# x enters the y product in fp32 as it was loaded, and conditioning matrices are fetched by index in every block

## The chip, the cores and the metric

The kernel runs on one core of a Trainium2 chip. The metric is the device time of one execution in microseconds, the median over several runs. The engines of the core are named as in the profile: PE is the matrix engine (TensorE; "PEld" is its weight load), DVE is VectorE, ACT is ScalarE, POOL is GpSimd, SP is the sync engine, which here only issues DMAs.

## The reference

Everything is fp32. B = 64 batches, C = D = 64, T = 1024, 4 experts of rank 8.

```python
y    = einsum('bct,bcd->bdt', x, W[condition])        # W is [16, 64, 64], one matrix for each batch
base = y @ W_up.T                                     # W_up is [1024, 1024]
top1 = argmax(y @ gate_w.T + expert_bias)             # 4 experts
z    = einsum('nh,erh->ner', y, lora_A)               # rank 8
out  = x + base + (z[top1] @ lora_B[top1].T) * 1.0
```

## The kernel before, in words

**Blocks.** The 64 batches are worked on in 16 blocks of four. A block is two row groups t = 0 and 1 of two batches each; a row group of x is 128 partitions (two batches of 64 channels) by 1024 columns. Block 0 is written out by hand in the start-up, together with the preparation of the weights. Blocks 1 to 14 are a loop of seven rounds with two blocks each (`in_blocks`), and block 15, the closing one, follows it. `q` is the number of a block, `par` its parity, and `x_sb` holds x for two blocks.

**The big product.** y @ W_up.T is done in 2x2 form with seven products in place of eight (a11, a12, a22, s1, s2, s3, s4). An operand is split into a high part, rounded to fp32r by ACT (`round_...`, L446), and a low part, the difference, made by DVE (`low_operand`, L873); a product (`multiply`, L680) is three fp32r matmuls for each of four slices. The operands a11, a12, a21, a22 are quarters of y, and s1 to s4 are sums and differences of them, which POOL makes (L286 to L299). DVE adds each product to x in `x_sb` (L960, L964), and SP stores the result. `route` (DVE, small instructions) picks the expert, `turn_z` (L695) transposes the picked z on PE, ACT copies it, and `add_delta` (L686) adds the low-rank term.

**y of the next block.** During block q, PE makes y of block q + 1 in four pieces, `make_y(q + 1, t, h)`, L613 to L622: piece (0,0) after product s2, (0,1) after s1, (1,0) after s3, (1,1) after s4. Their order among the products is written out by hand in the PE's `period`. In the kernel before they go like this:

- x is split into `x_hl`. ACT rounds it to fp32r (`split_x`, L432, one instruction of 64x1024 for each batch), and DVE makes the low part (L863), which lands on the other 64 partitions. So for each batch the 128 partitions of `x_hl` are high and low part of the same 64 channels.
- All 16 conditioning matrices lie in SBUF as `cond_hl`, high and low part side by side, made once in the start-up (L511, L1020).
- PE reads the condition of the batch into a register (`load_index`, L610), and this register picks the matrix in `cond_hl`. A piece is eight fp32r matmuls of 128 columns, `x_hl` as the stationary operand.
- Each batch leaves its result in two column halves that have to be added: ACT copies one to `y_small` (L436), and DVE adds the other (`sum_y`, L868) and so writes a11, a12, a21 or a22.

PE waits before piece (t,0) for `x_low` (DVE's split), and before every piece until the piece before it has been summed out of `y_ps`.

**Block 0 and block 1** get their y in another way (`make_first_y`, L624 to L631): SP fetches the conditioning matrices of two batches by index into a block-diagonal 128x128 tile (`load_first_cond`, L303 to L311), and PE multiplies `x_sb` as loaded, in fp32, by that tile: four matmuls of 128 columns, and ACT copies the bank out (L441).

**Queues.** SP issues the stores of a block in the order c11, c12, c21, c22, each behind a wait for DVE. ACT issues the loads of x for block q + 1 (`load_x`) at the start of block q, each behind a wait for the stores of block q - 1.

Of the kernel before, what the change touches and what calls it, by code (L numbers as in the profile page):

```python
# [5 lines left out]
def adaln_ffn_kernel(  # L6
# [55 lines left out]
    cond_rows = cond_weights.rearrange("s c d -> c s d")  # L62
# [7 lines left out]
    with ctx:  # L70
# [12 lines left out]
        cond_hl = sb("cond_hl", [P, S, 2, D], fp32r)  # L83
# [6 lines left out]
        x_hl = sb("x_hl", [P, 2, 2, T], fp32r)  # L90
        y_small = sb("y_small", [P, BANK], fp32)
# [25 lines left out]
        cond_sb = raw.enter_context(nc.sbuf_tensor("cond_sb", [P, S, D], fp32))  # L117
# [17 lines left out]
        cond_loaded = [sem(f"cond_loaded{h}") for h in range(2)]  # L135
        first_zero = sem("first_zero")
        first_loaded = [sem(f"first_loaded{t}") for t in range(4)]
# [8 lines left out]
        cond_high = sem("cond_high")  # L146
        cond_low = sem("cond_low")
# [7 lines left out]
        x_high = sem("x_high")  # L155
        x_low = sem("x_low")
        y_done = sem("y_done")
        y_small_out = sem("y_small_out")
# [33 lines left out]

        def is_last(q):
            return isinstance(q, int) and q == BLOCKS - 1
# [7 lines left out]
        def halves_of(bank):  # L202
            return bank[:, :, :].rearrange("q n (g a d) -> q (n g) a d", a=2, d=D)
# [5 lines left out]

        def first_cond(t):  # L210
            return y_small[:, t * P:(t + 1) * P]
# [90 lines left out]
        def _(sp):  # L302
            def load_first_cond(t):  # L303
                sp.wait_ge(index_loaded, 16)
                sp.wait_ge(first_zero, 1)
# [15 lines left out]
            load_first_cond(0)  # L321
# [5 lines left out]
            load_first_cond(1)  # L327
# [5 lines left out]
            load_first_cond(2)  # L333
            load_first_cond(3)
# [9 lines left out]
            def period(q, par, closing):  # L344
                sp.wait_ge(c11_out, q + 1)
# [22 lines left out]
        def _(pool):  # L368
# [5 lines left out]
            pool.memset(y_small[:, :], 0.0).then_inc(first_zero, 1)  # L374
# [38 lines left out]
        def _(act):  # L413
# [12 lines left out]
            def split_x(q, par, t, used, halves=(0, 1)):  # L426
                act.wait_ge(x_loaded[2 * par + t], 8 * (q - par) + 16)
                if used:
                    act.wait_ge(y_done, 4 * q - 2 + 2 * t)
                for b in halves:  # L430
                    rows = slice(b * C, (b + 1) * C)
                    act.activation(x_hl[rows, t, b, :], x_sb[rows, 2 * par + t, :], ACT.Copy).then_inc(x_high, 1)  # L432
# [75 lines left out]
            def round_cond():  # L508
                for h in range(2):
                    act.wait_ge(cond_loaded[h], 16)  # L510
                act.activation(cond_hl[:, :, 0, :], cond_sb[:, :, :], ACT.Copy).then_inc(cond_high, 1)  # L511

# [35 lines left out]
            round_cond()  # L548
# [9 lines left out]
            act.wait_ge(cond_low, 1)  # L558
# [19 lines left out]
            def period(q, par, closing):  # L578
# [5 lines left out]
                else:  # L584
# [23 lines left out]
        def _(pe):  # L608
            def load_index(q, t):
                return [pe.value_load(index_sb[0:1, bass.ds(4 * q + 2 * t + b, 1)], min_val=0, max_val=S - 1)  # L610
                        for b in range(2)]
# [557 lines left out]
```

## Time and profile before

| | |
|---|---|
| median of three runs | 432.45 us (432.19 to 432.79) |
| span of the profiled execution, first to last instruction | 430.5 us (430.454) |
| median less span | 2.0 us |
| busy share: PE, DVE, ACT, POOL | 99%, 83%, 44%, 27% |
| chain that ended last | PE 93% of it, `y_ps` L620 11% |
| one block of the loop | 25.2 us |
| granted TensorE clock | 1.00, full speed (2.4 GHz), in all blocks |

No time of its own is given for the profiled execution, only its span; the 2.0 us between it and the median lie around the span. A row of a timeline gives the start and the duration of merged instructions in us. Matmuls overlap in the pipeline, so the time that a group of them takes on PE is read from its start to the start of the next group, and is shorter than the printed duration.

### The profile page before, as it was taken

Reading aid. Unit: us, or ns where it says so; the run is one execution under the profiler, and the core shown is the slowest. Engines: PE = TensorE matmul, PEld = TensorE weight load, DVE = VectorE, ACT = ScalarE, POOL = GpSimd, SP = SyncE. Lnnn points to the kernel's source line nnn. Section 1 sums busy time; section 2 is a strip of 40 time slices with the busy share of each in tenths; the row PEclk is TensorE's granted clock in tenths of the full one; section 3 lists DMA queues with packets and bytes.
Section 4 is the critical chain, followed back from the end, with each engine's and each line's share of the span. In section 5 each row is a group of like instructions: output and inputs, shape, how many; then the busy total and the mean of one; then the engine's idle time right before and its main releaser. Section 6 shows DMA issues by size and latency. Waiting matters only on the chain.

```text
span 430.5 us, 8609 instructions
## 1 busy us (share of the span) xinstructions
PE 424.8 (99%) x2937; PEld 396.7 (92%) x2938; DVE 358.1 (83%) x648; ACT 191.5 (44%) x302; POOL 117.5 (27%) x92
## 2 busy tenths in 40 slices
PE   8999999999999999999999999999999999999997
PEld 7989999999999999999999999999999999999996
DVE  3998489697979979797997979799797989979773
ACT  4873463362625336262543636254263625426220
POOL 4971040503205050220505023050502305050230
DMA  7930140402214041230503123050312305031202
GB/s 266 350 57 3 48 151 24 151 33 90 96 41 154 24 129 41 90 105 32 163 24 124 46 78 117 24 171 24 122 49 72 123 24 171 24 122 49 80 19 97
DMA packets 18583, 38.85 MB, mean 90 GB/s; under 512 B 5095, under 2 KB 5351, under 8 KB 18571
## 3 DMA queue, kind: packets, MB, share of 16 engines
q1 hardware_dynamic: 14336, 23.86, 15.8%
q10 hardware_dynamic: 4234, 14.83, 11.4%
q8 instruction: 7, 0.11, 0.1%
q14 instruction: 6, 0.04, 0.0%
HBM read 21.91 MB, written 16.78 MB: 90 GB/s over the span
## 4 chain that ended last, share of the span: by engine, by line
PE 93%; ACT 3%; DMA 2%; DVE 1%; SPq 0%; issue 0%; DVEq 0%
PE bank_x L680 23%; PE bank_y L680 23%; PE bank_c L680 20%; PE y_ps L620 11%; PE bank_b L680 10%; DMA w_raw<-in_L_ffn_W_up_dram 2%; PE bank_x L686 1%; PE bank_y L686 1%; PE bank_b L686 1%; PE bank_c L686 1%; PE y_ps L628 1%; ACT w_s L493 1%; ACT w_a L493 1%; PE bank_y L717 1%; PE bank_y L663 1%; PE bank_c L695 1%
## 5 line engine op out<-in xcount | busy, mean ns | idle before, releaser
L286 POOL TENSOR_TENSOR s_sum<-a 128x512 f32<-128x512 f32 x15 | 19.5, 1301 | 283.3 <-DVE a L868 264.8
L432 ACT ACTIVATE x_hl<-x_sb 64x1024 fp32r<-64x1024 f32 x56 | 59.1, 1055 | 34.0 <-DMA out_dram<-x_sb 29.4
L863 DVE TENSOR_TENSOR x_hl<-x_sb,x_hl 64x1024 fp32r<-64x1024 f32 x56 | 68.4, 1221 | 1.7
L436 ACT ACTIVATE y_small<-y_ps 128x512 f32<-128x512 f32 x56 | 33.5, 598 | 57.7 <-PE y_ps L620 57.7
L620 PE MATMUL y_ps<-cond_hl,x_hl 128*128 x448 | 58.1, 273 | 0.0
L620 PEld LDWEIGHTS y_ps<-cond_hl,x_hl 128*128 128x128 f32 x448 | 54.7, 191 | 1.5
L680 PE MATMUL bank_x<-w_a,hl_a 128*128 128x256 f32 (+1 forms) x408 | 54.2, 288 | 0.0
L680 PEld LDWEIGHTS bank_x<-w_a,hl_a 128*128 128x128 f32 x408 | 52.9, 188 | 0.4
L868 DVE TENSOR_TENSOR a<-y_ps,y_small 128x512 f32<-128x512 f32 x56 | 38.5, 687 | 16.7 <-ACT y_small L436 16.7
L680 PE MATMUL bank_y<-w_s,hl_s 128*128 128x292 f32 (+1 forms) x384 | 51.6, 290 | 0.0
L680 PE MATMUL bank_x<-w_s,hl_s 128*128 128x292 f32 (+1 forms) x384 | 51.5, 290 | 0.0
L680 PE MATMUL bank_y<-w_a,hl_a 128*128 128x292 f32 (+1 forms) x384 | 51.0, 288 | 0.0
L680 PEld LDWEIGHTS bank_y<-w_s,hl_s 128*128 128x128 f32 x384 | 49.9, 188 | 0.8 <-issue 0.2
L680 PEld LDWEIGHTS bank_x<-w_s,hl_s 128*128 128x128 f32 x384 | 49.8, 188 | 0.6
L680 PEld LDWEIGHTS bank_y<-w_a,hl_a 128*128 128x128 f32 x384 | 49.6, 188 | 0.1
L680 PE MATMUL bank_c<-w_s,hl_s 128*128 128x512 f32 x192 | 48.2, 399 | 0.0
L680 PE MATMUL bank_b<-w_s,hl_s 128*128 128x512 f32 x192 | 48.2, 400 | 0.0
L446 ACT ACTIVATE hl_a<-a 128x512 fp32r<-128x512 f32 x48 | 30.5, 636 | 36.1 <-DVE a L868 33.6
L680 PEld LDWEIGHTS bank_c<-w_s,hl_s 128*128 128x128 f32 x192 | 34.9, 188 | 7.3
L680 PEld LDWEIGHTS bank_b<-w_s,hl_s 128*128 128x128 f32 x192 | 35.2, 190 | 6.8
L680 PE MATMUL bank_c<-w_a,hl_a 128*128 128x512 f32 x168 | 41.2, 394 | 0.0
L873 DVE TENSOR_TENSOR hl_s<-s_sum,hl_s 128x512 fp32r<-128x512 f32 x32 | 37.8, 1188 | 4.0 <-ACT hl_s L446 3.1
(120 smaller groups left out, 566.0 us busy)
## 6 DMA issues: line engine op xcount, KB each, us to landing
out_dram<-x_sb SPq DMA_DIRECT2D x63, 256.0 KB, 2.0
x_sb<-in_x_dram ACTq DMA_DIRECT2D x28, 512.0 KB, 3.7
w_raw<-in_L_ffn_W_up_dram SPq DMA_DIRECT2D x8, 512.0 KB, 7.5
x_sb<-in_x_dram SPq DMA_DIRECT2D x4, 512.0 KB, 8.8
cond_sb<-in_L_cond_weights_dram SPq DMA_DIRECT2D x2, 256.0 KB, 10.1
out_dram<-x_sb SPq DMA_DIRECT2D x2, 128.0 KB, 1.9
router_sb<-in_L_ffn_lora_A_dram ACTq DMA_DIRECT2D x1, 128.0 KB
lora_b_sb<-in_L_ffn_lora_B_dram SPq DMA_DIRECT2D x1, 128.0 KB, 7.8
```

Of the source, the lines that this page charges most:

```text
L286: eng.tensor_tensor(s1_sum[:, :], a21[:, :], a22[:, :], ALU.add).then_inc(s1_added, 1)
L432: act.activation(x_hl[rows, t, b, :], x_sb[rows, 2 * par + t, :], ACT.Copy).then_inc(x_high, 1)
L436: act.activation(y_small[:, :].rearrange("q (g d) -> q g d", d=D), halves_of(y_ps)[:, :, 1, :], ACT.Copy).then_inc(y_small_out, 1)
L446: act.activation(hl[op][:, 0, :, :], src[:, :].rearrange("q (k n) -> q k n", n=P), ACT.Copy)\
L493: act.activation(turn_target(op, c, 0), bank.rearrange("q (k n) -> q k n", n=P), ACT.Copy)\
L620: mm = pe.matmul(y_ps[:, k % KH // 2, at:at + P], x_hl[:, t, b, k * P:(k + 1) * P], cond_hl[:, index[b], :, :], start=True, stop=True)
L628: mm = pe.matmul(FIRST_Y[2 * t + h][:, k * P:(k + 1) * P], x_sb[:, t, (h * KH + k) * P:(h * KH + k + 1) * P], first_cond(t), start=True, s ...
L680: mm = pe.matmul(dst, hl[op][:, a, k, :], w[:, b, k, cols], start=(fresh and k == 0 and a + b == 0), stop=(k == KH - 1 and a == 1), skip_g ...
L686: return pe.matmul(dst, z_t[t][:, :], src, start=False, stop=True, skip_group_check=True)
L863: dve.tensor_tensor(x_hl[other, t, b, :], x_sb[rows, 2 * par + t, :], x_hl[rows, t, b, :].bitcast(fp32), ALU.subtract).then_inc(x_low, 1)
L868: dve.tensor_tensor(dst[:, :].rearrange("q (g d) -> q g d", d=D), halves_of(y_ps)[:, :, 0, :], y_small[:, :].rearrange("q (g d) -> q g d", ...
L873: dve.tensor_tensor(hl[op][:, 1, :, :], src[:, :].rearrange("q (k n) -> q k n", n=P), hl[op][:, 0, :, :].bitcast(fp32), ALU.subtract).then ...
```

## The change

The y of every block is made as that of the first two: x as loaded, in fp32, times a block-diagonal pair of conditioning matrices. The split of x (ACT and DVE), the register loads on PE, the resident `cond_hl` with its loads and splits, and the sum over halves on DVE are gone. The 128x128 tiles now lie in `cond_pair`, four of them (two blocks, two row groups), cleared once by POOL. SP fetches the four matrices of block q + 1 at the start of its `period` for block q, so behind the stores of block q - 1 and ahead of those of block q. A piece of y is four fp32 matmuls; PE waits before piece (t,0) for x and for the pair, and before every piece until all pieces but the last one have been moved. ACT moves a piece out of `y_ps` directly (`move_y`).

```diff
-        x_hl = sb("x_hl", [P, 2, 2, T], fp32r)
-        y_small = sb("y_small", [P, BANK], fp32)
+        cond_pair = sb("cond_pair", [P, 4, P], fp32)
...
 # SyncE
+            def load_pair(q, par, t):
                 for b in range(2):
                     rows = slice(b * C, (b + 1) * C)
-                    index = sp.value_load(index_sb[0:1, 2 * t + b:2 * t + b + 1], min_val=0, max_val=S - 1)
-                    sp.dma_start(first_cond(t)[rows, b * D:(b + 1) * D],
+                    index = sp.value_load(index_sb[0:1, bass.ds(4 * q + 2 * t + b, 1)], min_val=0, max_val=S - 1)
+                    sp.dma_start(cond_pair[rows, 2 * par + t, b * D:(b + 1) * D],
                                  cond_weights[bass.ds(index, 1), :, :].rearrange("s c d -> (s c) d"))\
-                       .then_inc(first_loaded[t], 16)
+                       .then_inc(pair_loaded[2 * par + t], 16)
+            def load_next_pair(q, par, t):
+                sp.wait_ge(y_done, 4 * q + 2 * t - 6)
+                load_pair(q, par, t)
...
             sp.dma_start(x_sb[:, 2, :], x_pairs[2]).then_inc(x_loaded[2], 16)
-            sp.dma_start(cond_sb[0:C, :, :], cond_rows).then_inc(cond_loaded[0], 16)
             sp.dma_start(x_sb[:, 3, :], x_pairs[3]).then_inc(x_loaded[3], 16)
-            sp.dma_start(cond_sb[C:2 * C, :, :], cond_rows).then_inc(cond_loaded[1], 16)
...
             def period(q, par, closing):
+                if q_next(q):
+                    load_next_pair(q + 1, 1 - par, 0)
+                    load_next_pair(q + 1, 1 - par, 1)
                 sp.wait_ge(c11_out, q + 1)
                 store(q, par, 0, 0)
 # ScalarE
-            def split_x(q, par, t, used, halves=(0, 1)):
...
-            def move_small_y(q, t, h):
+            def move_y(q, t, h, to):
                 act.wait_ge(y_done, 4 * q + 2 * t + h + 1)
-                act.activation(y_small[:, :].rearrange("q (g d) -> q g d", d=D), halves_of(y_ps)[:, :, 1, :],
-                               ACT.Copy).then_inc(y_small_out, 1)
+                act.activation(to[:, :], y_ps[:, h, :], ACT.Copy).then_inc(y_summed, 1)
...
-            round_cond()
-            act.wait_ge(cond_low, 1)
...
-                    split_x(q + 1, 1 - par, 0, True)
                 round_s4(q, True)
                 round_s3(q, True)
-                if not closing:
-                    split_x(q + 1, 1 - par, 1, True)
                 move_z(q, par, 0, True)
                 if not closing:
-                    move_small_y(q + 1, 0, 0)
+                    move_y(q + 1, 0, 0, a11)
                     round_a11(q + 1, True)
-                    move_small_y(q + 1, 0, 1)
+                    act.wait_ge(low["s4"], q + 1)
+                    move_y(q + 1, 0, 1, a12)
                     round_a12(q + 1, True)
-                    move_small_y(q + 1, 1, 0)
+                    move_y(q + 1, 1, 0, a21)
                 move_z(q, par, 1, True)
                 if not closing:
-                    move_small_y(q + 1, 1, 1)
+                    move_y(q + 1, 1, 1, a22)
                     round_a22(q + 1, True)
 # TensorE
-            def load_index(q, t):
...
-            def make_y(q, t, h, index):
+            def make_y(q, par, t, h):
                 if h == 0:
-                    pe.wait_ge(x_low, 4 * q + 2 * t - 6)
-                pe.wait_ge(y_summed, 4 * q + 2 * t + h)
-                for k in range(h * KH, (h + 1) * KH):
-                    for b in range(2):
-                        at = (k % 2) * 2 * P + b * P
-                        mm = pe.matmul(y_ps[:, k % KH // 2, at:at + P], x_hl[:, t, b, k * P:(k + 1) * P],
-                                       cond_hl[:, index[b], :, :], start=True, stop=True)
+                    pe.wait_ge(x_loaded[2 * par + t], 8 * (q - par) + 16)
+                    pe.wait_ge(pair_loaded[2 * par + t], 16 * (q - par) + 32)
+                pe.wait_ge(y_summed, 4 * q + 2 * t + h - 1)
+                for k in range(KH):
+                    mm = pe.matmul(y_ps[:, h, k * P:(k + 1) * P],
+                                   x_sb[:, 2 * par + t, (h * KH + k) * P:(h * KH + k + 1) * P],
+                                   cond_pair[:, 2 * par + t, :], start=True, stop=True)
                 mm.then_inc(y_done, 1)
 # VectorE
-            def split_x(q, par, t, b):
-            def sum_y(dst, q, t, h):
-            def split_cond():
...
```

## Rows read from the trace of the kernel before

**Rows 1.** The page, busy time, share and instructions of each engine.
```profile
PE 424.8 (99%) x2937; PEld 396.7 (92%) x2938; DVE 358.1 (83%) x648; ACT 191.5 (44%) x302; POOL 117.5 (27%) x92
```

**Rows 2.** Windows of blocks 2, 8 and 15: length, busy by engine, clock, DMA.
```profile
77.52:103.05 25.52, 25.52 (x173) 23.61 (x172) 21.48 (x39) 11.18 (x18) 5.91 (x4) 1.00 0.25 84
...
229.04:254.25 25.20, 25.20 (x173) 23.54 (x172) 21.87 (x39) 11.30 (x18) 6.25 (x4) 1.00 0.25 83
...
405.45:430.45 25.00, 22.17 (x153) 20.51 (x151) 15.46 (x33) 3.88 (x8) 5.85 (x4) 1.00 0.20 74
```

**Rows 3.** Timeline of PE in block 8, the four pieces (L620) and what follows.
```profile
240.91 1.00 PE L620 MATMUL y_ps<-cond_hl,x_hl 128*128 x8
...
241.80 3.00 PE L680 MATMUL bank_b<-w_s,hl_s 128*128 128x512 f32 x12
...
244.88 1.00 PE L620 MATMUL y_ps<-cond_hl,x_hl 128*128 x8
245.72 3.24 PE L680 MATMUL bank_x<-w_s,hl_s 128*128 128x292 f32 x24
248.80 1.06 PE L620 MATMUL y_ps<-cond_hl,x_hl 128*128 x8
249.69 3.01 PE L680 MATMUL bank_c<-w_s,hl_s 128*128 128x512 f32 x12
...
252.77 0.27 PE L695 MATMUL bank_y<-ident,z_parts 128*128 128x128 f32 x1
...
254.02 0.39 PE L686 MATMUL bank_b<-lora_b_hl,z_t 128*128 128x512 f32 x1
```

**Rows 4.** Timeline of PE in the start-up, pieces of y in fp32 (L628).
```profile
12.94 1.06 PE L628 MATMUL y_ps<-y_small,x_sb 128*128 128x128 f32 x8
13.83 0.60 PE L663 MATMUL bank_b<-ident,w_raw 128*128 128x128 f32 x4
...
27.37 0.60 PE L663 MATMUL y_ps<-ident,w_raw 128*128 128x128 f32 x4
27.72 3.01 PE L680 MATMUL bank_b<-w_s,hl_s 128*128 128x512 f32 x12
...
42.04 1.06 PE L628 MATMUL y_ps<-y_small,x_sb 128*128 128x128 f32 x8
42.85 3.04 PE L680 MATMUL bank_c<-w_s,hl_s 128*128 128x512 f32 x12
...
50.83 0.27 PE L695 MATMUL bank_y<-ident,z_parts 128*128 128x128 f32 x1
...
52.07 0.39 PE L686 MATMUL bank_b<-lora_b_hl,z_t 128*128 128x512 f32 x1
```

**Rows 5.** Timelines of DVE and PE in block 2, around piece (1,0).
```profile
96.17 1.22 DVE L863 TENSOR_TENSOR x_hl<-x_sb,x_hl 64x1024 fp32r<-64x1024 f32 x1
...
97.53 1.12 PE L620 MATMUL y_ps<-cond_hl,x_hl 128*128 x8
```

**Rows 6.** Timelines of PE and DVE in block 15, around product s2.
```profile
408.46 3.20 PE L680 MATMUL bank_x<-w_a,hl_a 128*128 128x292 f32 x24
411.67 3.27 PE L680 MATMUL bank_y<-w_s,hl_s 128*128 128x292 f32 x24
414.79 0.33 PE L695 MATMUL bank_c<-ident,z_parts 128*128 128x128 f32 x1
...
410.29 2.92 DVE L873 TENSOR_TENSOR hl_s<-s_sum,hl_s 128x512 fp32r<-128x512 f32 x2 [0.83 <-ACT hl_s L446]
```

**Rows 7.** The page, DVE's sum of y: count, busy us, mean ns, idle before.
```profile
L868 DVE TENSOR_TENSOR a<-y_ps,y_small 128x512 f32<-128x512 f32 x56 | 38.5, 687 | 16.7 <-ACT y_small L436 16.7
```

**Rows 8.** Timeline of SP: a pair fetched, stores in block 8; landing of pairs.
```profile
10.04 1.72 SPq L309 DMA_DIRECT2D y_small<-in_L_cond_weights_dram  x2
...
230.83 0.91 SPq L337 DMA_DIRECT2D out_dram<-x_sb  x2
...
DMA to landing us min/median/max: 2.4/5.9/7.0
```

More of the change, by code:

```diff
@@ L116, in adaln_ffn_kernel @@
         raw.enter_context(nc.sbuf_tensor("raw_rest", [P, KH * 2 * GC - OC * ER], fp32))
-        cond_sb = raw.enter_context(nc.sbuf_tensor("cond_sb", [P, S, D], fp32))
         raw.close()
@@ L134, in adaln_ffn_kernel @@
         bias_zero = sem("bias_zero")
-        cond_loaded = [sem(f"cond_loaded{h}") for h in range(2)]
-        first_zero = sem("first_zero")
-        first_loaded = [sem(f"first_loaded{t}") for t in range(4)]
+        pair_zero = sem("pair_zero")
+        pair_loaded = [sem(f"pair_loaded{s}") for s in range(4)]
         index_loaded = sem("index_loaded")
@@ L191, in in_blocks, with q_next @@
             period(BLOCKS - 1, (BLOCKS - 1) % 2, True)
+        def q_next(q):
+            return not isinstance(q, int) or 0 < q < BLOCKS - 1
         def is_last(q):
@@ L320, in _ @@
             load_w_up(4)
-            load_first_cond(0)
+            load_first_pair(0, 0)
             sp.dma_start(x_sb[:, 0, :], x_pairs[0]).then_inc(x_loaded[0], 16)
@@ L326, in _ @@
             load_w_up(1)
-            load_first_cond(1)
+            load_first_pair(0, 1)
             sp.dma_start(x_sb[:, 1, :], x_pairs[1]).then_inc(x_loaded[1], 16)
             sp.dma_start(x_sb[:, 2, :], x_pairs[2]).then_inc(x_loaded[2], 16)
-            sp.dma_start(cond_sb[0:C, :, :], cond_rows).then_inc(cond_loaded[0], 16)
             sp.dma_start(x_sb[:, 3, :], x_pairs[3]).then_inc(x_loaded[3], 16)
-            sp.dma_start(cond_sb[C:2 * C, :, :], cond_rows).then_inc(cond_loaded[1], 16)
-            load_first_cond(2)
-            load_first_cond(3)
+            load_first_pair(1, 0)
+            load_first_pair(1, 1)
             def store(q, par, t, half):
@@ L373, in _ @@
             pool.memset(bias_sb[:, :], 0.0).then_inc(bias_zero, 1)
-            pool.memset(y_small[:, :], 0.0).then_inc(first_zero, 1)
+            pool.memset(cond_pair[:, :, :], 0.0).then_inc(pair_zero, 1)
             for e in range(E):
@@ L424, in load_x @@
                 act.dma_start(x_sb[:, 2 * par + t, :], x_pairs[2 * q + t]).then_inc(x_loaded[2 * par + t], 16)
-            def split_x(q, par, t, used, halves=(0, 1)):
[L427 to L432, printed above, removed]
-            def move_small_y(q, t, h):
+            def move_y(q, t, h, to):
                 act.wait_ge(y_done, 4 * q + 2 * t + h + 1)
-                act.activation(y_small[:, :].rearrange("q (g d) -> q g d", d=D), halves_of(y_ps)[:, :, 1, :],
-                               ACT.Copy).then_inc(y_small_out, 1)
+                act.activation(to[:, :], y_ps[:, h, :], ACT.Copy).then_inc(y_summed, 1)
             def move_first_y(n, to):
@@ L506, in move_z @@
                 act.activation(z_t[t][:, :], src, ACT.Copy).then_inc(z_ready, 1)
[L508 to L511, printed above, removed]
             act.wait_ge(ident_done, 1)
@@ L625, in make_first_y @@
                 pe.wait_ge(x_loaded[t], 16)
-                pe.wait_ge(first_loaded[t], 32)
+                pe.wait_ge(pair_loaded[t], 32)
                 for k in range(KH):
                     mm = pe.matmul(FIRST_Y[2 * t + h][:, k * P:(k + 1) * P],
-                                   x_sb[:, t, (h * KH + k) * P:(h * KH + k + 1) * P], first_cond(t),
+                                   x_sb[:, t, (h * KH + k) * P:(h * KH + k + 1) * P], cond_pair[:, t, :],
                                    start=True, stop=True)
@@ L821, in period @@
                 multiply("a11", q, chain, True)
-                index = [None, None]
-                if not closing:
-                    index[0] = load_index(q + 1, 0)
                 pe.wait_ge(c21_out, q)
@@ L832, in period @@
                 if not closing:
-                    make_y(q + 1, 0, 0, index[0])
+                    make_y(q + 1, 1 - par, 0, 0)
                     pe.wait_ge(p4_out, q)
@@ L839, in period @@
                 if not closing:
-                    make_y(q + 1, 0, 1, index[0])
+                    make_y(q + 1, 1 - par, 0, 1)
                 pe.wait_ge(u2_out, q + 1)
@@ L843, in period @@
                 if not closing:
-                    index[1] = load_index(q + 1, 1)
-                    make_y(q + 1, 1, 0, index[1])
+                    make_y(q + 1, 1 - par, 1, 0)
                 multiply("s4", q, bank_c, True)
@@ L851, in period @@
                 else:
-                    make_y(q + 1, 1, 1, index[1])
+                    make_y(q + 1, 1 - par, 1, 1)
                     pe.wait_ge(u3_out, q + 1)
@@ L859, in _ @@
         def _(dve):
-            def split_x(q, par, t, b):
-                rows, other = slice(b * C, (b + 1) * C), slice((1 - b) * C, (2 - b) * C)
-                dve.wait_ge(x_high, 4 * q + 2 * t + b - 7)
-                dve.tensor_tensor(x_hl[other, t, b, :], x_sb[rows, 2 * par + t, :],
-                                  x_hl[rows, t, b, :].bitcast(fp32), ALU.subtract).then_inc(x_low, 1)
-            def sum_y(dst, q, t, h):
-                dve.wait_ge(y_small_out, 4 * q + 2 * t + h - 7)
-                dve.tensor_tensor(dst[:, :].rearrange("q (g d) -> q g d", d=D), halves_of(y_ps)[:, :, 0, :],
-                                  y_small[:, :].rearrange("q (g d) -> q g d", d=D), ALU.add).then_inc(y_summed, 1)
             def low_operand(op, src, q):
@@ L1016, in after_delta22 @@
                 add_bank(bank_b, par, 1, 1).then_inc(c22_out, 1)
-            def split_cond():
-                dve.wait_ge(cond_high, 1)
-                dve.tensor_tensor(cond_hl[:, :, 1, :], cond_sb[:, :, :], cond_hl[:, :, 0, :].bitcast(fp32),
-                                  ALU.subtract).then_inc(cond_low, 1)
             split_turned("s4", 2)
@@ L1067, in _ @@
             low_operand("s4", a12, 0)
-            split_cond()
             after_p6(0, 0)
@@ L1104, in period @@
                 if not closing:
-                    for b in range(2):
-                        split_x(q + 1, 1 - par, 0, b)
                     after_p4(q, par)
@@ L1113, in period @@
                 else:
-                    sum_y(a11, q + 1, 0, 0)
-                    split_x(q + 1, 1 - par, 1, 0)
                     low_operand("a11", a11, q + 1)
@@ L1119, in period @@
                 if not closing:
-                    sum_y(a12, q + 1, 0, 1)
-                    split_x(q + 1, 1 - par, 1, 1)
                     low_operand("a12", a12, q + 1)
@@ L1124, in period @@
                 route(q, 1)
-                if not closing:
-                    sum_y(a21, q + 1, 1, 0)
                 after_delta12(q, par)
                 if not closing:
-                    sum_y(a22, q + 1, 1, 1)
                     after_delta21(q, par)
```

21 lines of the change are left out of this document (4 added, 17 removed).

## The prediction

> **What bounds the kernel now.** I read the page's engine line first: PE is busy 424.8 of 430.5 us, DVE 83%, ACT 44% [rows 1]. Then the windows, block by block: in a block of the loop PE is busy for its whole length, 25.20 of 25.20 us, at a granted clock of 1.00, which is the upper level, 2.4 GHz [rows 2]. So what counts is what PE does in its own stream, and the few places where it waits. Busy time hides such waits here, because a matmul's printed duration covers its neighbour's start. I therefore take the time of a piece of y from its start to the start of the next group, in the timeline [rows 3]. Two places stand out in the windows: block 2 takes 25.52 us where block 8 takes 25.20, and in the closing block PE is busy only 22.17 of 25.00 us [rows 2].
>
> The change takes four instructions for each row group from DVE and two from ACT. None of that shortens the kernel by itself: DVE and ACT are not the bound. It counts only where PE waits for them.
>
> **The change, part by part.**
>
> *The pieces of y on PE.* Before, a piece is eight matmul records. The four pieces of block 8 take: (0,0) with the transpose of z behind it, 241.80 - 240.91 = 0.89 us; (0,1) 245.72 - 244.88 = 0.84; (1,0) 249.69 - 248.80 = 0.89; and (1,1) with the transpose ahead of it and a pair of delta matmuls behind it, 254.02 - 252.77 = 1.25 [rows 3]. That is 3.87 us for each block.
>
> The new piece has the same form as the pieces of the start-up, which are in the trace: four fp32 matmuls of 128 columns, that show as eight records, x_sb the stationary operand [rows 4]. So halving the number of matmuls in the code does not halve the work. With a product behind, such a piece takes 42.85 - 42.04 = 0.81 us; with a fp32 transpose behind, 13.83 - 12.94 = 0.89; and from the transpose of z over piece and delta pair it is 52.07 - 50.83 = 1.24 [rows 4]. A transpose ahead of a product costs little of its own: four take 27.72 - 27.37 = 0.35, so three at 0.11 and the last 0.03 [rows 4]. The product behind a fp32 piece starts up some 0.03 us slower (s4's duration is 3.04 us behind a fp32 piece, 3.01 behind the other form [rows 3, 4]). The four places after the change:
> - (0,0): 0.89 + 0.03 = 0.92, against 0.89: +0.03
> - (0,1): 0.81 + 0.03 = 0.84, against 0.84: 0
> - (1,0): 0.81 + 0.03 = 0.84, against 0.89: -0.05
> - (1,1): 1.24 against 1.25: -0.01
>
> The sum is -0.03 us for a block, and 14 blocks (1 to 14) make such pieces: 14 x 0.03 = -0.4 us. These are differences of hundredths, so I bound the term by 0 and by twice its size, -0.8.
>
> The precision page of the Trainium skill (FP8 and Floating Point Precision, TensorE Precision Notes) says that true fp32 takes four passes through the array, where reduced fp32 takes one, which speaks against this change. The trace does not show it as time for this shape: the fp32 piece takes 0.81 us, the one before 0.84. By the pass count alone, half the matmuls with four passes each would double the array's work in the pieces.
>
> *Block 2.* It is 25.52 - 25.20 = 0.32 us longer than block 8 [rows 2]. At piece (1,0) DVE's last half of the split of x ends at 96.17 + 1.22 = 97.39 and PE starts the piece at 97.53 [rows 5]; in the code the piece waits for that split (`x_low`). With the split gone PE waits for the loaded x only, which is what the split itself had to have before it. I take the full -0.3 us; the other bound is 0.
>
> *The closing block.* Product a12 there takes 411.67 - 408.46 = 3.21 us, and a11 ahead of it, the same 24 matmuls, 408.46 - 405.45 = 3.01 [rows 2, 6]. Behind a12 comes s2 with no a22 between, and its low part is made by DVE only from 410.29 on, after 0.83 us of waiting for ACT's rounding, which waits for POOL's s1 and s2, and these for the last piece of y [rows 6]. s2 then takes 414.79 - 411.67 = 3.12, another 0.11 too much. Now ACT's copy is the last step of y and DVE's addition, 0.69 us [rows 7], falls out of this chain, so the low part comes about 0.7 us earlier, more than the 0.3 us that PE loses. What is late next is the transpose of z, which needs DVE's routing behind the low parts; it moves forward with them. I take -0.3 us, bounds 0 and -0.4.
>
> *The start-up.* Two 256 KB loads and a rounding and a split of 128x1024 go. In the code they are issued behind all of W_up and behind x of row groups 0 to 2, so nothing that PE needs early is queued behind them; I count 0, and as bounds one stall of the size of block 2's, -0.3, and +0.1.
>
> *SP.* Four fetches for each block. SP has nothing to do between the last store of block 7, issued by 230.83 + 0.91 = 231.74 [rows 8], and the first of block 8, which comes only behind s1 and the first delta pair, so close to 244.88, where the piece behind them starts [rows 3]. Two fetches take 1.72 us from issue to issue's end, and with the register load ahead of the first some 2.5 [rows 8]: 5 us for the four, all in that gap. Queued behind them is only that store. The pair for (0,*) is issued by 234.3; in the start-up such a fetch landed 2.4 to 7.0 us after issue, median 5.9, behind the loads of W_up [rows 8]. So it lands between 236.7 and 241.3, most likely near the lower end since only two stores are ahead of it; PE wants it at 240.91 [rows 3]. The second pair is issued by 236.8 and wanted at 248.80. Cost 0; at the upper bound of 7.0 it would be 0.4 us in each block.
>
> The DMA page of the Trainium skill (DMA: Bandwidth & Descriptors, Anatomy of one DMA) gives about 2.0 us as the fixed cost of one DMA on another path than this; 2.4 us, the fastest here, is near it, and by that figure no pair would be late.
>
> *ACT's copy, PE's waits, register loads.* The copy is as long as that to `y_small`, and hidden. PE has one more semaphore wait for each row group and two register loads fewer; its sequencer runs ahead of the array, 0.
>
> **Sum.** -0.4 - 0.3 - 0.3 = -1.0 us: a span of 430.5 - 1.0 = 429.5, and with the 2.0 us around it, against the median of 432.45, 431.4 us. As a ratio it is -0.23%. The measurement tells about 0.2% (0.9 us) from no change, so the forecast lies just past that bound. The case's own range comes from the term bounds, not all at an end together: 430.9 to 432.1.
>
> **The rivals.**
> - *Nothing that can be told.* The pieces come out equal in the blocks, and only one of the two stalls goes; 0 to -0.5 us, 432.2. For it: the piece term is a sum of hundredths and one of its four parts is positive. Against it: both stalls have their cause in the removed work. Chance 0.24.
> - *The pairs come late.* The mechanism is the landing on SP's queue, behind two stores. It decides from a landing of 6.6 us on (234.3 + 6.6 = 240.9); at 7.0 it is 0.4 us in each of 14 blocks: +5.6 - 1.0, so 437. Against it is the missing W_up traffic. Chance 0.05.
> - *fp32 costs its passes.* A one-pass matmul of the piece takes 0.84 / 8 = 0.105 us; four times that for four matmuls is 1.68, +0.84 for each of 56 pieces: +47 us, 479. The rows of the start-up exclude it nearly: 0.01. (By the rule of the precision page.)
> - *PE's sequencer loses its lead* at three waits in a row ahead of (t,0), where two stood: if each shows as some 0.1 us, a record's pace, it costs 28 x 0.1 = +2.8 against -1.0, 434.3. Against it: with two waits the pieces show nothing of that size. Chance 0.06.
> - *A larger gain.* Every term comes at its lower bound: -0.8 in the pieces, -0.3 in block 2, -0.4 in the closing block, -0.3 in the start-up, together -1.8 us, 430.6. For it: DVE, with 56 x 1.22 = 68 us [rows 5] and 38.5 us [rows 7] less to do, is in time everywhere. Chance 0.09.
>
> That leaves 0.55 for the forecast.
>
> **Chances and range.** The forecast's case falls past -0.9 us in about three of five: 0.34; with the larger gain 0.43, and some of the no-change case's spread makes it 0.46. Slower: 0.05 + 0.01 + 0.06 and 0.01 of spread, 0.13. Same: 0.41. The range for 8 in 10: down past the larger gain, 430.3, up past no change, 432.9; what it leaves out is the three slower rivals and a little of the spread at both ends, under 0.2.
>
> **What would show it.** PE in a middle block: 25.17 us for 25.20; piece (0,1) to its product 0.81; (0,0) with the transpose 0.92. Block 2 as long as the others. In block 15, a12 3.0 us. `cond_pair` landings of 2 to 4 us, and no wait of PE for them. DVE's busy share near 58% ((358.1 - 68 - 38.5) / 430). The prediction is wrong if the eight records of a fp32 piece pace at another step than 0.11 us in the loop, if the 0.3 us of block 2 stay (then it is not the split), or if blocks carry a new wait for `cond_pair` or x.

## The result: 431.08 us, 1.2 us less than before

The changed kernel takes 431.08 us (median of 16 runs, 430.94 to 432.29), the kernel before 432.26 (16 runs). The ratio is 0.9971, 95% interval 0.9961 to 0.998. The profiled execution has a span of 429.3 us against 430.5, at a granted clock of 1.00.

The page of the changed kernel, busy time and share by engine, then the times from issue to landing of SP's fetches:

```profile
PE 423.2 (99%) x2937; PEld 395.8 (92%) x2937; DVE 264.4 (62%) x535; ACT 134.3 (31%) x245; POOL 113.4 (26%) x92
...
cond_pair<-in_L_cond_weights_dram SPq DMA_DIRECT2D x64, 16.0 KB, 2.6
```

DVE has 94 us less to do than in [rows 1] and ACT 57, and the kernel is 1.2 us shorter; PE has as many instructions as before. The windows of blocks 2, 8 and 15 of the changed kernel, with the columns of [rows 2]:

```profile
77.41:102.58 25.17, 25.17 (x173) 23.48 (x172) 15.25 (x32) 7.21 (x14) 5.92 (x4) 1.00 0.26 88
228.43:253.60 25.17, 25.17 (x173) 23.51 (x172) 15.24 (x32) 7.28 (x14) 5.92 (x4) 1.00 0.26 86
404.63:429.28 24.65, 21.85 (x153) 20.45 (x151) 15.08 (x32) 3.94 (x8) 5.84 (x4) 1.00 0.20 75
```

So block 2 is 0.35 us shorter, block 8 0.03, and the closing block 0.35. Read from the first product of a block to that of the next, all 14 blocks of the loop now take 25.16 to 25.18 us, where before 13 of them took 25.19 to 25.22 and block 2 25.52. The difference of the spans, 1.17 us, is made up as: start-up up to block 1, 52.30 to 52.25, -0.05; block 2 -0.355; the other 13 blocks together -0.41; closing block -0.35.

The timeline of PE in block 8 of the changed kernel answers to [rows 3]:

```profile
240.29 1.05 PE L593 MATMUL y_ps<-cond_pair,x_sb 128*128 128x128 f32 x8
241.18 0.27 PE L669 MATMUL bank_c<-ident,z_parts 128*128 128x128 f32 x1
241.21 2.99 PE L654 MATMUL bank_b<-w_s,hl_s 128*128 128x512 f32 x12
...
244.28 1.05 PE L593 MATMUL y_ps<-cond_pair,x_sb 128*128 128x128 f32 x8
245.08 3.28 PE L654 MATMUL bank_x<-w_s,hl_s 128*128 128x292 f32 x24
248.20 1.05 PE L593 MATMUL y_ps<-cond_pair,x_sb 128*128 128x128 f32 x8
249.01 3.04 PE L654 MATMUL bank_c<-w_s,hl_s 128*128 128x512 f32 x12
...
252.12 0.27 PE L669 MATMUL bank_y<-ident,z_parts 128*128 128x128 f32 x1
...
253.37 0.40 PE L660 MATMUL bank_b<-lora_b_hl,z_t 128*128 128x512 f32 x1
```

From starts: piece (0,0) with the transpose 0.92 us, (0,1) 0.80, (1,0) 0.81, and the group around (1,1) 1.25. Before they were 0.89, 0.84, 0.89 and 1.25 [rows 3]. Only (1,0) keeps a gain: the product behind (0,1) takes 248.20 - 245.08 = 3.12 where it took 248.80 - 245.72 = 3.08, which gives the gain of (0,1) back. Of (1,0)'s own 0.08 us the product s4 behind it gives back 0.03: both together take 252.12 - 248.20 - 0.23 = 3.69 us, where they took 252.77 - 248.80 - 0.23 = 3.74 (0.23 is the delta matmul between s4 and the transpose). The closing block, PE's timeline, answers to [rows 6]:

```profile
404.63 3.19 PE L654 MATMUL bank_y<-w_a,hl_a 128*128 128x292 f32 x24
407.66 3.19 PE L654 MATMUL bank_x<-w_a,hl_a 128*128 128x292 f32 x24
410.68 3.19 PE L654 MATMUL bank_y<-w_s,hl_s 128*128 128x292 f32 x24
413.71 0.27 PE L669 MATMUL bank_c<-ident,z_parts 128*128 128x128 f32 x1
413.74 3.00 PE L654 MATMUL bank_b<-w_s,hl_s 128*128 128x512 f32 x12
```

a12 takes 3.02 us in place of 3.21, s2 3.03 in place of 3.12, and the transpose of z, up to the product behind it, 0.03 in place of 0.10. These three make up the 0.35 us.

### The profile page after: what moved, and what is told of

It is laid out like the page before. It is cut to its first block, busy times and chain, and to the rows that moved or that the text cites. A ratio compares the mean times of both kernels' runs of the same rounds, so it can differ in the third digit from the quotient of the medians.

```text
span 429.3 us, 8491 instructions
## 1 busy us (share of the span) xinstructions
PE 423.2 (99%) x2937; PEld 395.8 (92%) x2937; DVE 264.4 (62%) x535; ACT 134.3 (31%) x245; POOL 113.4 (26%) x92
## 4 chain that ended last, share of the span: by engine, by line
PE 93%; ACT 3%; DMA 2%; DVE 1%; SPq 0%; issue 0%; DVEq 0%
PE bank_x L654 23%; PE bank_y L654 23%; PE bank_c L654 19%; PE y_ps L593 12%; PE bank_b L654 10%; DMA w_raw<-in_L_ffn_W_up_dram 2%; PE bank_y L660 1%; PE bank_x L660 1%; PE bank_b L660 1%; PE bank_c L660 1%; PE y_ps L602 1%; ACT w_s L480 1%; ACT w_a L480 1%; PE bank_y L691 1%; PE bank_y L637 1%; ACT lora_b_hl L478 0%
## 5 line engine op out<-in xcount | busy, mean ns | idle before, releaser
L831 DVE TENSOR_TENSOR hl_a<-a,hl_a 128x512 fp32r<-128x512 f32 x49 | 39.5, 806 | 41.6 <-ACT hl_a L433 41.6
L593 PE MATMUL y_ps<-cond_pair,x_sb 128*128 128x128 f32 x448 | 59.0, 275 | 0.0
L424 ACT ACTIVATE a<-y_ps 128x512 f32<-128x512 f32 x56 | 33.4, 597 | 80.1 <-PE y_ps L593 80.1
L593 PEld LDWEIGHTS y_ps<-cond_pair,x_sb 128*128 128x128 f32 x448 | 54.6, 191 | 1.3
L831 DVE TENSOR_TENSOR hl_s<-s_sum,hl_s 128x512 fp32r<-128x512 f32 x32 | 48.4, 1548 | 0.3 <-ACT hl_s L433 0.2
L922 DVE TENSOR_TENSOR x_sb<-bank_c,x_sb 128x512 f32<-128x512 f32 x30 | 20.7, 691 | 33.2 <-PE bank_c L660 26.3
L918 DVE TENSOR_TENSOR x_sb<-bank_y,x_sb 128x512 f32<-128x512 f32 x39 | 26.7, 684 | 16.4 <-PE bank_y L660 8.5
L654 PEld LDWEIGHTS bank_c<-w_a,hl_a 128*128 128x128 f32 x168 | 30.6, 188 | 6.1
```

What stands on the lines that cost most here:

```text
L424: act.activation(to[:, :], y_ps[:, h, :], ACT.Copy).then_inc(y_summed, 1)
L593: mm = pe.matmul(y_ps[:, h, k * P:(k + 1) * P], x_sb[:, 2 * par + t, (h * KH + k) * P:(h * KH + k + 1) * P], cond_pair[:, 2 * par + t, :], ...
L654: mm = pe.matmul(dst, hl[op][:, a, k, :], w[:, b, k, cols], start=(fresh and k == 0 and a + b == 0), stop=(k == KH - 1 and a == 1), skip_g ...
L831: dve.tensor_tensor(hl[op][:, 1, :, :], src[:, :].rearrange("q (k n) -> q k n", n=P), hl[op][:, 0, :, :].bitcast(fp32), ALU.subtract).then ...
L918: return dve.tensor_tensor(wide(x_part(par, t, half)), bank[:, :, 0:QUARTER], wide(x_part(par, t, half)), ALU.add)
L922: return dve.tensor_tensor(x_part(par, t, half), bank[:, 0, :], x_part(par, t, half), ALU.add)
```

## The experiments

The table gives for each run the length of block 2, of the other 13 blocks of the loop, and of the closing block, from its trace, in us. The start-up is left out of it: in all but one of these traces the first loop block begins between 52.2 and 52.6 us, whatever the edit, so differences of 0.3 us in a span can come from there. The exception is e7. The kernel before was run again beside each set of experiments: 432.28 us beside e1 to e4, 432.35 beside e5 to e8, 432.30 beside e9 to e12. Ratios are to these.

| run | block 2 | other blocks | closing | median (runs) |
|---|---|---|---|---|
| before | 25.52 | 25.19 to 25.22 | 25.00 | 432.26 (16) |
| changed | 25.17 | 25.16 to 25.18 | 24.65 | 431.08 (16) |
| e1 before, no split | 25.17 | 25.14 to 25.20 | 25.01 | 431.91 (10) |
| e2 before, no index | 26.29 | 25.17 to 25.21 | 24.99 | 432.83 (1) |
| e3 changed, split and wait back | 25.17 | 25.16 to 25.18 | 24.65 | 431.25 (10) |
| e4 changed, split back | 25.17 | 25.16 to 25.18 | 24.66 | 431.16 (1) |
| e5 changed, one DVE step in y's chain | 25.17 | 25.16 to 25.18 | 25.02 | 431.59 (10) |
| e6 changed, half the columns | 25.15 | 25.15 to 25.21 | 24.66 | 431.02 (1) |
| e7 changed, double the columns | 28.55 | 28.54 to 28.55 | 24.66 | 482.03 (1) |
| e8 changed, pairs behind a22 | 26.72 | 26.72 to 27.14 | 24.66 | 454.66 (1) |
| e9 before, split ahead of the sums | 26.96 | 26.19 to 26.36 | 25.01 | 446.99 (4) |
| e10 changed, splits and sums back | 26.26 | 25.19 to 25.22 | 25.02 | 432.94 (10) |
| e11 changed, pairs behind a12 | 25.18 | 25.16 to 25.18 | 24.65 | 431.17 (1) |
| e12 changed, other start-up order | 25.17 | 25.16 to 25.17 | 24.66 | 431.39 (11) |

**e1: the kernel before without the split in the loop.**

```diff
-                    split_x(q + 1, 1 - par, 0, True)
...
+                    act.activation(x_hl[:, t, b, :]..., ident..., ACT.Copy)
...
-                    pe.wait_ge(x_low, 4 * q + 2 * t - 6)
+                    pe.wait_ge(x_loaded[2 * par + t], 8 * (q - par) + 16)
```

> The kernel before, with the split of x left out of the loop: x_hl is filled once in the start-up and the pieces of y multiply that, so y is not the reference's; PE waits for the loaded x in place of the split. Theory (PE waits for DVE's split): block 2 falls from 25.52 to 25.20 us or less, piece (1,0) from 0.87-0.90 to about 0.84-0.87, so the other blocks fall by up to 0.03; the closing block stays at 25.00, since the sum on DVE stays. Median about -0.6 us against before. Rival (the register loads on PE or the fp32r form make these times): block 2 stays at 25.5 and (1,0) as it is; no change in the median.

DVE's calls of `split_x` in the loop are gone as well. Ratio 0.9994 (0.9977 to 1.0012). The blocks say more than the median: PE's timeline around piece (1,0) of a middle block, and the window of block 2.

```profile
248.56 1.00 PE L621 MATMUL y_ps<-cond_hl,x_hl 128*128 x8
249.40 1.38 PE L681 MATMUL bank_c<-w_s,hl_s 128*128 128x512 f32 x5
```
```profile
77.75:102.92 25.17, 25.17 (x173) 23.48 (x172) 17.22 (x35) 7.14 (x14) 5.91 (x4) 1.00 0.24 85
```

With fp32r matmuls and resident matrices as before, and register loads too, (1,0) takes 0.84 us, block 2 25.17 and the mean block the same 25.17 as in the changed kernel. So the gain of the loop does not need the fp32 form. The closing block kept its 25.01. The median came 0.37 us lower (431.91 against 432.28) where I had expected 0.6: this profile's start-up was 0.26 us longer than that of before. That most likely comes from the experiment itself: the four added ACT instructions hold ACT for 3.89 us from 34.75 on, and the stretch of PE from 35.8 to 45.9 us, which they run beside, takes 10.16 us, where it takes 9.84 to 9.85 in every other trace.

**e2: the kernel before without register loads.**

```diff
-                                       cond_hl[:, index[b], :, :], start=True, stop=True)
+                                       cond_hl[:, b, :, :], start=True, stop=True)
```

> The kernel before, with the register loads on PE left out: each batch uses matrix 0 or 1 of the resident set, so y is not the reference's. Theory: nothing moves, block 2 stays at 25.52, (1,0) at 0.87-0.90, the block at 25.20, the closing block at 25.00. Rival (register loads cost): (1,0), which follows a load, falls to 0.84, blocks by 0.03 or more.

I had expected no change; outside block 2, piece (1,0) fell to 0.84 to 0.88, and the blocks to a mean of 25.18, half of the way to 25.17. So the registers, the loads or the addressing with them, have a part in the 0.03 us for each block, but only together with the late split: in e1 and in e9 (below) they stand as before, the split is gone or early, and (1,0) takes 0.84 in every block. This is one execution. Block 2 went up to 26.29, which says what sort of stall this is. ACT's timeline there: it waited 4.03 us for a store to land before it could issue the load of x that stands ahead of the split in its queue.

```profile
85.84 0.34 ACTq L424 DMA_DIRECT2D x_sb<-in_x_dram  x1
86.31 2.15 ACT L432 ACTIVATE x_hl<-x_sb 64x1024 fp32r<-64x1024 f32 x2 [4.03 <-DMA out_dram<-x_sb]
```

The stall of block 2 is thus not a fixed 0.3 us. It is how far stores that land late, in one execution, push the splits of x past PE's need. In the kernel before too it stands at both row groups. DVE's timeline, then PE's, at piece (0,0) of block 2:

```profile
86.77 2.47 DVE L863 TENSOR_TENSOR x_hl<-x_sb,x_hl 64x1024 fp32r<-64x1024 f32 x2
```
```profile
89.38 1.11 PE L620 MATMUL y_ps<-cond_hl,x_hl 128*128 x8
```

The split ends at 89.24, 0.14 us ahead of the piece; in the blocks after it, it ends 0.88 ahead. Piece (0,0) and the two groups behind it are 0.15 us longer than in the other blocks, and s3 with (1,0) 0.17 us.

**e3 and e4: the split back in the changed kernel, with and without PE's wait.**

```diff
+                    split_x(q + 1, 1 - par, 0)            # ACT and DVE, at their old places
...
                     pe.wait_ge(pair_loaded[2 * par + t], 16 * (q - par) + 32)
+                    pe.wait_ge(x_low, 4 * q + 2 * t - 6)  # e3 only
```

> The changed kernel with the split of x put back on ACT and DVE, into a tile that no product reads, and with PE waiting for it before pieces (0,0) and (1,0), as before. Theory: block 2 goes from 25.17 back to 25.5, (1,0) longer by some 0.03-0.07 in each block; the closing block stays at 24.65, because no sum on DVE is in its chain. Median +0.6 to +0.9 us against the changed kernel. Rival (the fp32 form made the gain): blocks stay at 25.17.

> The same as the run with the wait, but PE does not wait for the split: only the work is back on ACT and DVE. Theory: the load alone costs nothing, all blocks 25.17, closing 24.65 to 24.7. Rival (it was the load of ACT and DVE, through a shared port or late low parts): blocks longer, up to 25.2, block 2 up to 25.5, closing up to 25.0.

e4 came as expected: no change. e3 did not: ratio 0.9978 (0.9965 to 0.9992), and not one block longer, though PE waits for the split as it did before. My theory up to here, that the wait for the split is what costs, falls in this form. DVE's timeline of e3 with PE's shows why; the last two lines are DVE's and PE's in block 8 of the kernel before:

```profile
191.65 1.22 DVE L846 TENSOR_TENSOR x_hl<-x_sb,x_hl 64x1024 fp32r<-64x1024 f32 x1
...
195.16 1.22 DVE L846 TENSOR_TENSOR x_hl<-x_sb,x_hl 64x1024 fp32r<-64x1024 f32 x1
```
```profile
197.80 1.05 PE L607 MATMUL y_ps<-cond_pair,x_sb 128*128 128x128 f32 x8
```
```profile
247.38 1.22 DVE L863 TENSOR_TENSOR x_hl<-x_sb,x_hl 64x1024 fp32r<-64x1024 f32 x1
```
```profile
248.80 1.06 PE L620 MATMUL y_ps<-cond_hl,x_hl 128*128 x8
```

The last half of the split ends at 196.38, 1.4 us ahead of the piece. In the kernel before it ended at 248.60 for the piece at 248.80, 0.2 us ahead, and in block 2 at 97.39 for a piece at 97.53 [rows 5]. The difference of 1.2 us is what the two sums of y that stood ahead of it in DVE's queue take there, at 0.6 us from start to start. The new theory: splits are late because they are queued behind sums, which wait for PE and ACT. e9 and e10 test it.

**e5: one DVE step put back into the chain of the last piece.**

```diff
-                    move_y(q + 1, 1, 1, a22)
+                    act.activation(y_hop[:, :], y_ps[:, 1, :], ACT.Copy).then_inc(y_hop_out, 1)
...
+                    dve.tensor_tensor(a22[:, :], y_hop[:, :], y_hop[:, :], ALU.max).then_inc(y_summed, 1)
```

> The changed kernel with one DVE instruction of 128x512 put back into the chain of the last piece: ACT copies piece (1,1) into a tile, DVE copies that into a22. Theory (closing term: DVE's addition in the chain y, s1, s2, rounding, low part): the closing block goes from 24.65 back to 24.9-25.0, product a12 there from 3.02 to about 3.2; all other blocks 25.17. Median +0.3 us. Rival (the closing gain came from DVE having less to do overall): closing stays at 24.65.

```profile
407.75 3.18 PE L657 MATMUL bank_x<-w_a,hl_a 128*128 128x292 f32 x24
410.98 3.27 PE L657 MATMUL bank_y<-w_s,hl_s 128*128 128x292 f32 x24
414.10 0.33 PE L672 MATMUL bank_c<-ident,z_parts 128*128 128x128 f32 x1
```

The closing block is 25.02 us again, a12 3.23, s2 3.12, and all other blocks 25.17. The ratio, 0.9986 (0.9957 to 1.0015), is too wide to show it, the trace does: one instruction of 0.69 us in the chain from the last piece over s1 and s2 to the low part costs 0.37 us there, and nothing in the loop, where a22 stands between a12 and s2.

**e6 and e7: half and double the moving columns.**

```diff
-                                   cond_pair[:, 2 * par + t, :], start=True, stop=True)
+                                   cond_pair[:, 2 * par + t, 0:D], start=True, stop=True)                # e6, output slice to match
+                                   cond_pair[:, 2 * par + t, :].unsqueeze(1).to_broadcast([P, 2, P]), ...)  # e7, likewise
```

> The changed kernel with 64 moving columns in place of 128 in each matmul of the loop's pieces (half of y left out, so the output is not the reference's). Theory (the weight load sets the pace of a record): records stay 0.111 us apart, a piece 0.80, blocks within 0.1 us of 25.17. Rival (the passes set it: two of 128 columns for each record are 0.107 us at 2.4 GHz): records 0.055-0.06 apart, a piece about 0.45, block 23.7, median -20 us.

> The changed kernel with 256 moving columns in each matmul of the loop's pieces (the pair's tile twice; the writes overlap in the bank, so y is not the reference's). Theory (weight load of 0.111 us, or the stream where it is longer): a record at 256 columns takes two passes of 256, 0.21 us, so a piece about 1.7 us and a block 25.17 + 4 x 0.9 = 28.8. Rival (a record is one pass): 256 columns are 0.107 us, records stay near 0.12 apart, a block about 25.3.

PE's timeline of e6, piece (1,0), and then of e7, piece (0,0), each with what follows:

```profile
248.21 1.00 PE L593 MATMUL y_ps<-cond_pair,x_sb 128*128 128x64 f32 x8
249.02 3.05 PE L654 MATMUL bank_c<-w_s,hl_s 128*128 128x512 f32 x12
```
```profile
210.47 1.89 PE L594 MATMUL y_ps<-cond_pair,x_sb 128*128 128x256 f32 x8
212.20 0.27 PE L670 MATMUL bank_c<-ident,z_parts 128*128 128x128 f32 x1
```

Half the columns leave the piece at 0.81 us: the stream of columns is not what paces a record of 64 or 128 columns. The weight load, one for each record, is the candidate; it was not varied by itself. Double the columns make the piece ahead of the transpose 1.73 us where it was 0.89, and the pieces with a product or a delta pair behind them 1.54 where they were 0.81. A record then takes 0.216 us, which at 2.4 GHz is the time of about 512 columns, 256 twice. The Trainium skill (FP8 and Floating Point Precision, TensorE Precision Notes) gives four passes for true fp32. The trace agrees: two passes for each of the two records of a matmul. By that count, an estimate, the passes take 0.107 us for a record at 128 columns, and hide within the 0.111 us that a record takes with 64 columns as well. With twice the columns a block is 3.4 us longer: 3.0 in the pieces, the rest in what stands behind them. I had expected 3.6. The 482 us of e7 also hold a start-up 3.6 us longer, ahead of all that the edit touches: PE waits 1.8 us there for a load of W_up, and then the granted clock is 0.50, the level of 1.2 GHz, from 10.5 to 13.0 us, where it is 1.00 throughout in the changed kernel.

**e8 and e11: the pairs fetched later.**

```diff
                 if q_next(q):
+                    sp.wait_ge(product_done["a22"], q + 1)      # e8; "a12" in e11
                     load_next_pair(q + 1, 1 - par, 0)
```

> The changed kernel with SP waiting for product a22 of the block before it fetches the pairs. a22 ends 8.9 us into a block, the first pair is issued 2.5 us later and lands 2.4-2.6 us after that, at 14.0; PE wants it at 12.1. Theory: every block has a wait of some 1.9 us at piece (0,0), block about 27.1, median +26 us. Rival (the pairs are hidden anyway, or land faster): no change.

> The changed kernel with SP waiting for product a12 of the block, 6.1 us into it, before it fetches the pairs. First pair issued by 8.6, landed by 11.2, wanted at 12.1. Theory: no wait, blocks 25.17. With the run behind a22 this brackets the point from which lateness costs. Rival (landing 3.5 us or more): blocks 25.2 to 25.8.

```profile
200.26 1.15 PE L594 MATMUL y_ps<-cond_pair,x_sb 128*128 128x128 f32 x8 [1.28 <-DMA cond_pair<-in_L_cond_weights_dram]
```

Behind a22, which ends 8.8 us into a block, blocks are 1.5 to 2.0 us longer, all of it at piece (0,0); behind a12, which ends at 6.1, nothing is lost. In the changed kernel the first fetch is issued 2.8 us into the block (231.24 - 228.43, SP's timeline):

```profile
231.24 4.52 SPq L295 DMA_DIRECT2D cond_pair<-in_L_cond_weights_dram  x4
```

With the register load ahead of it that is a start at about 1.8. So a delay of some 4.3 us is free, and one of 7.0 costs 1.5 to 2.0: the room is about 5 us.

**e9: the kernel before, split ahead of the sums.**

```diff
-                    sum_y(a11, q + 1, 0, 0)
                     split_x(q + 1, 1 - par, 1, 0)
+                    split_x(q + 1, 1 - par, 1, 1)
+                    sum_y(a11, q + 1, 0, 0)
                     low_operand("a11", a11, q + 1)
...
                     sum_y(a12, q + 1, 0, 1)
-                    split_x(q + 1, 1 - par, 1, 1)
```

> The kernel before with two moves in DVE's order alone: both halves of the split for row group 1 go ahead of the sum for a11 (they stood behind the sums for a11 and a12, which wait for a piece of y and for ACT's copy). New theory (it is not the split's work nor PE's wait for it, but that the split stands in DVE's queue behind the sums): the last half ends some 2 us before piece (1,0), (1,0) takes 0.84 in all blocks, blocks 25.17, block 2 25.17 to 25.2, closing block unchanged at 25.00; median about -0.7 us against before. Rival (the split's own length, or the load of DVE): blocks stay at 25.20 and block 2 at 25.5.

It is slower by 3.4% (1.0319 to 1.0351). DVE's timeline, then PE's:

```profile
223.89 2.47 DVE L863 TENSOR_TENSOR x_hl<-x_sb,x_hl 64x1024 fp32r<-64x1024 f32 x2
226.39 0.69 DVE L868 TENSOR_TENSOR a<-y_ps,y_small 128x512 f32<-128x512 f32 x1
```
```profile
225.95 0.40 PE L686 MATMUL bank_x<-lora_b_hl,z_t 128*128 128x256 f32 x2
227.14 1.11 PE L620 MATMUL y_ps<-cond_hl,x_hl 128*128 x8 [0.79 <-DVE a L868]
228.09 3.12 PE L680 MATMUL bank_y<-w_s,hl_s 128*128 128x292 f32 x23
```

The forecast of -0.7 us was wrong, though one part of it held: (1,0) takes 0.84 us in every block. But the sum for a11 now ends at 227.08, and PE waits for it before piece (0,1), since both banks of `y_ps` are read by one sum: about 1 us in each block. The order of before was pinned from both sides, the sum by piece (0,1) and the split by (1,0), with no room for 2.4 us between.

**e10: splits and sums back, in the fp32 form.**

```diff
-                pe.wait_ge(y_summed, 4 * q + 2 * t + h - 1)
+                pe.wait_ge(y_summed, 4 * q + 2 * t + h)
...
+                    hop_y(a11, q + 1, 0, 0)               # DVE, 128x512, for each piece at the old sum's place
+                    split_x(q + 1, 1 - par, 1, 0)
...
```

> The changed kernel in fp32, with the split back (PE waits for it) and with a DVE instruction of 128x512 for each piece at the place and in the order of the old sums. New theory (sums ahead of splits on DVE make them late; the form of the matmul is neutral): (1,0) longer than 0.81 by 0.02 to 0.06, blocks 25.20, block 2 25.3 to 25.5, closing 25.0: the time of before, median 432.3. Rival (the fp32 form is what made it robust): blocks at 25.17.

Beside what is shown, PE's wait for `x_low` is back as in e3, and ACT's wait for s4's low part ahead of the copy of piece (0,1), which only the changed kernel has, is gone. Ratio 1.0013 (0.9998 to 1.0027). Windows of blocks 2, 8 and 15, then PE's timeline in block 2:

```profile
77.49:103.75 26.26, 25.69 (x173) 23.57 (x172) 21.89 (x39) 11.27 (x18) 6.24 (x4) 1.00 0.26 84
229.75:254.96 25.20, 25.20 (x173) 23.55 (x172) 21.90 (x39) 11.28 (x18) 6.24 (x4) 1.00 0.26 86
406.19:431.21 25.02, 22.17 (x153) 20.50 (x151) 15.45 (x33) 3.93 (x8) 5.85 (x4) 1.00 0.20 74
```
```profile
89.86 1.16 PE L608 MATMUL y_ps<-cond_pair,x_sb 128*128 128x128 f32 x8 [0.35 <-DVE x_hl L847]
```

All three gains are gone: blocks 25.20, (1,0) 0.85, closing 25.02, and a stall in block 2, here 1.1 us, at the splits of both row groups. Two waits of PE are back at (1,0), for the split and for the sum of the piece before. It is the split that ends last: in the middle blocks 0.19 us ahead of the piece, the sum 1.44 us. So with splits and sums the loop takes the time of before in either form of the matmul, and each block is 0.03 us shorter without the split in fp32r (e1), and with the split but without the sums in fp32 (e3). The closing block's part was taken out and put back in the fp32 form only (e5); a fp32r kernel without the sum was not run.

Block 2 is less clear. In e10 DVE stands idle there before the split of the first row group:

```profile
87.33 2.47 DVE L847 TENSOR_TENSOR x_hl<-x_sb,x_hl 64x1024 fp32r<-64x1024 f32 x2 [1.33 <-ACT x_hl L432]
```

So it is not a sum that holds this split up, but ACT, which waited 3.96 us for a store and could issue its load of x only at 85.77; in e3's profile that load went out at 83.50. How e3 would fare with stores as late as these, its trace doesn't show. Its ten executions speak for no stall in most: 8 have a span of 429.2 to 429.4 us. Those of e10 would be near 430.0 without a stall in block 2 (an estimate from the other blocks and the closing one), and 6 of 10 are 430.9 or more.

**e12: an attempt at a faster one.** PE has one stall left in the changed kernel that DVE causes, 0.36 us in the start-up before the last transposes for a22.

```diff
-            split_turned("s2", 1)
-            low_operand("s2", s2_sum, 0)
             subtract(dve, 4, 3)
+            split_turned("s2", 1)
+            low_operand("s2", s2_sum, 0)
```

> The changed kernel with DVE's last subtraction of W_up quarters (for the transpose a22, 3, which PE waits for at 31.9 us in the start-up) ahead of the last split of s2 and the low part of s2. Theory: PE's stall of 0.36 us there goes, and s2's product does not become late: span 428.9 to 429.0, median -0.3 us against the changed kernel. Rival: s2's low part becomes the bound instead, and nothing is won.

```profile
30.55 0.60 PE L637 MATMUL bank_c<-ident,w_raw 128*128 128x128 f32 x4
31.66 0.66 PE L637 MATMUL y_ps<-ident,w_raw 128*128 128x128 f32 x4 [0.51 <-DVE w_s L852]
```

Neither theory had it right. The stall did not go, it moved forward and grew: from the transposes at 30.55 to the next it is 1.11 us, four at a pace of 0.11 would be 0.44, and these next ones need a bank of `y_ps` that the moved split of s2 frees. The ratio to before is 0.998 (0.9971 to 0.9989), no better than the changed kernel, and the start-up is 0.24 us longer than there.

## Why the prediction was right

- *The sum.* Predicted -1.0 us on the span, measured -1.17; predicted 431.4 us, measured 431.08, in the range. As a ratio -0.29% against -0.23%. Two of the three terms, block 2 and the closing block, came from waits that the prediction had named and that the experiments bear out. The third had the right size for another reason.
- *Pieces on PE*, -0.03 us for a block: measured 25.20 to 25.17, -0.41 over 13 blocks. The total is right, its parts are not: all of it is (1,0), and e1 shows that to be the end of a wait and not a cheaper piece. The prediction took the 0.89 us of (1,0) as the price of the form and did not ask why (0,1), the same form, took 0.84. That +0.03, 0, -0.05 and -0.01 added up to the measured sum is in part luck. That eight records cost the same in both forms held: (1,0) and s4 together take 3.69 us in fp32 (changed) and in fp32r (e1).
- *Block 2*, -0.3: measured -0.35. That the split is behind it is right (e1). The reason was incomplete: it named piece (1,0) alone, where only half of the stall stands, the other half being at (0,0). What starts it is a store that lands late and holds up ACT's load and split of x (e2, e10); it was 0.3 us in one execution and 1.1 in two others. With the split back but no sums (e3) there was no stall; how much of that is the shorter queue on DVE and how much a store that landed earlier, the runs don't separate.
- *Closing block*, -0.3: measured -0.35, and e5 brings 0.37 of it back with one instruction. The shift of 0.7 us was more than the loss, as worked out, and the transpose of z moved forward too, 0.10 to 0.03 us, as foreseen.
- *Start-up*, 0: 52.30 to 52.25 us, within the 0.4 us by which start-ups differ here. Not shown to be anything else than 0.
- *SP*, 0: the four fetches are issued by 235.76, 7.3 us into the block, and land in 2.6; no wait of PE for them. The rival of late pairs was real in kind, with its point at some 5 us of delay (e8, e11), not reached.
- *fp32's passes*: the rival was rightly put at 0.01 for 128 columns, but only because a record takes that long with half the columns too; e7 shows the price.
- *DVE's share* was to be near 58%, and is 62%, 13 us more than worked out. The low parts of s1 and s2 take 1.55 us on average in place of 1.19, which is 11 of them; no run tests why. The blocks take their 25.17 us all the same.
- *The sequencer's lead*: one wait more for each row group shows nothing; each of the four pieces has the same length in all 14 blocks, within 0.001 us.

## What to carry to other kernels

Where PE is 99% busy, 94 us less work on DVE is worth only what PE waited for, and such waits do not show as idle time: compare the lengths of equal blocks and of equal groups from start to start, and look at the blocks that stand out. Then ask not only what the late instruction costs but what stands ahead of it in its queue and who pins that: moving it (e9) cost 15 us, while taking out the work ahead of it (e3 against e10) gained the 0.03 us of each block. At 128 moving columns, with new weights for every matmul, fp32 in four matmuls takes as long as fp32r in eight; at 256 the fp32 piece takes nearly twice as long (e7).

## What was not expected of the hardware

- A fp32 matmul shows as two records, 0.111 us apart at 64 (e6) and at 128 moving columns and 0.216 us at 256 (e7), at a clock of 1.00. In e6 only the first record of a piece is shorter, 0.057 us, and in the piece shown the gap behind the last record is longer by as much.
- The first product behind a fp32 piece starts slower than behind a fp32r piece by what the piece itself saves: (0,1) and s3 together take 3.92 us in both kernels.
- The time from issue to landing of the same 16 KB fetch: median 5.9 us behind large loads in the start-up [rows 8], 2.6 over the run of the changed kernel, 1.9 in e8, where SP issues it long after the last stores.
